# A three-layer decoder on one core: a deeper pipeline for the expert stage, and scatters that wait for products of attention

## The reference

```python
x = x + attn(layernorm(x))          # gated convolution over the 4 batches
x = x + xattn(layernorm(x), ctx)    # linear attention, 16 heads of 64, 128 features
x = x + ffn(layernorm(x))           # 8 experts, top 2
# ffn, for N = 2048 rows of 128:
routing = softmax(xf @ router_w.T); top_w, top_i = top_k(routing, 2)
top_w = top_w / sum(top_w)
h = silu(xf @ w_gate[e].T) * (xf @ w_up[e].T)     # 256 wide
out[n] = sum over the 2 chosen e of top_w * (h @ w_down[e].T)
```

## Time and profile before

| | |
|---|---|
| time, median of 3 runs | 307.88 us (306.1 to 310.2) |
| profiled execution, its own time | 305.2 us |
| its span, first to last instruction | 303.5 us |
| PE / PEld busy | 259.3 us (85%) / 221.1 us (73%) |
| DVE / ACT / POOL busy | 186.3 us (61%) / 162.4 us (54%) / 124.5 us (41%) |
| mean granted TensorE clock | 0.939 of full speed |

### The profile page before, as it was taken

How to read it: one execution, slowest core, us unless ns; L and a number is a source line. 1 busy time by engine, 2 the same in 40 slices (tenths; PEclk the granted TensorE clock), 3 DMA queues, 4 the chain that set the end, 5 groups by cost and what they waited for, 6 DMA issues and landing times.

```text
span 303.5 us, 5721 instructions
## 1 busy us (share of the span) xinstructions
PE 259.3 (85%) x1697; PEld 221.1 (73%) x1697; DVE 186.3 (61%) x713; ACT 162.4 (54%) x343; POOL 124.5 (41%) x183
## 2 busy tenths in 40 slices
PE   6999999999999999997999699778971899889700
PEld 3858686776889998995999488667861899889700
DVE  4678678696588888884888398757650222222206
ACT  2565564655777777773777366342530555445400
POOL 4648999441010001054104510711567466556520
PEclk9999999999999999999799979959996799999965
DMA  7999999940040000001000100257661688674048
GB/s 200 267 216 184 178 181 181 183 56 2 1 138 2 2 1 1 2 26 44 3 0 29 45 1 2 81 159 218 180 201 53 162 241 256 196 220 119 32 142 281
DMA packets 38446, 34.05 MB, mean 112 GB/s; under 512 B 3581, under 2 KB 31234, under 8 KB 38288
## 3 DMA queue, kind: packets, MB, share of 16 engines
q1 hardware_dynamic: 35312, 28.96, 43.3%
q0 software_dynamic: 2272, 4.24, 4.0%
q10 hardware_dynamic: 832, 0.49, 0.6%
HBM read 19.80 MB, written 14.32 MB: 112 GB/s over the span
## 4 chain that ended last, share of the span: by engine, by line
PE 68%; DVE 11%; issue 7%; another core or an unknown queue 5%; DMA 3%; POOL 2%; ACT 2%; ACTq 0%; POOLq 0%; DVEq 0%; SPq 0%
PE num L1294 15%; PE bank L1381 8%; PE num L1391 5%; PE bank L1255 5%; PE num L1233 4%; PE bank L246 4%; PE bank L248 4%; DVE X L929 4%; PE bank L247 4%; PE num L246 3%; PE num L248 2%; PE num L247 2%; PE bank L1166 2%; PE bank L1197 2%
## 5 line engine op out<-in xcount | busy, mean ns | idle before, releaser
L1294 PEld LDWEIGHTS num<-kvw_sb,q 128*128 128x128 f32 x512 | 70.3, 200 | 15.3 <-issue 8.6
L929 DVE SCALAR_TENSOR_TENSOR X<-num,rden,X 128x128 f32<-128x128 f32 x256 | 75.8, 342 | 4.6
L1294 PE MATMUL num<-kvw_sb,q 128*128 128x130 f32 x512 | 72.0, 286 | 7.0 <-DVE X L929 6.9
L666 ACT ACTIVATE relu_z<-bank 128x512 f32<-128x512 f32 x64 | 38.1, 595 | 32.6 <-PE bank L248 19.5
L546 POOL DMA_INDIRECT dispatched<-rows,slot_i x32 | 31.3, 977 | 51.1 <-DVE slot_i L1010 41.5
L566 POOL DMA_INDIRECT expert_out<-yo,xb x39 | 38.1, 977 | 29.2 <-issue 17.3
L1117 DVE TENSOR_TENSOR hid<-bank,silu_g 128x256 f32<-128x256 f32 x39 | 16.4, 422 | 51.2 <-ACT silu_g L694 31.2
L1381 PE MATMUL bank<-xT,wgu_sb 128*128 128x128 f32 x312 | 42.9, 282 | 2.3 <-issue 1.9
L583 ACT ACTIVATE q<-relu_z 128x512 f32<-128x512 f32 x64 | 40.4, 632 | 6.7 <-DVE acc L844 0.8
L1381 PEld LDWEIGHTS bank<-xT,wgu_sb 128*128 128x128 f32 x312 | 39.0, 196 | 3.0 <-issue 2.9
L1391 PE MATMUL num<-wd_sb,hid 128*128 x156 | 25.7, 288 | 12.0 <-issue 7.2
(11 more groups left out here) (173 smaller groups left out, 414.3 us busy)
## 6 DMA issues: line engine op xcount, KB each, us to landing
wgu_sb<-in_wgu SPq DMA_DIRECT2D x39, 256.0 KB
dispatched<-pad_row SPq DMA_DIRECT2D x3, 2795.0 KB, 35.4
xb<-dispatched SPq DMA_DIRECT2D x39, 65.0 KB
y_back<-expert_out SPq DMA_DIRECT2D x4, 512.0 KB, 4.9
wd_sb<-in_wd SPq DMA_DIRECT2D x1, 1024.0 KB, 4.8
out<-X SPq DMA_DIRECT2D x4, 256.0 KB, 2.5
X<-in_x SPq DMA_DIRECT2D x3, 256.0 KB, 6.6
expert_out<-yo,xb POOLq DMA_INDIRECT x39
```

The source lines that it names most:

```text
L666: a.activation(relu_z[:, k % 2, :], z_bank[k % 2], ACT.Relu).then_inc(relu_done, 1)
L929: ins = v.scalar_tensor_tensor(tile_of(n, t), banks[:, t // 2, t % 2, 0:P], rden[:, f % 2, t:t + 1], tile_of(n, t), ALU.mult, ALU.add)
L1294: last = nc.tensor.matmul(num[:, 2 * (h % 2) + t // 2, HA * (t % 2):HA * (t % 2 + 1)], q[:, h % 4, part], kvw_h, start=True, stop=True)
```

## The change

It has two parts.

**Scatters beside attention.** Each of the eight scatters of a round now waits for a product of attention: `after_head` waits either for the features of a head (`z_full`) or for the numerators that follow them (`num_done`). The half steps are counted from head 14 of batch n for the rounds of batches 0 and 1 (so the last ones fall into heads 0 to 3 of the next batch), and from head 10 for batch 2; PACE gives the half step of each scatter. The round of batch 3, in the expert stage, has no such wait, as before.

**Experts.** The gate and up products get two banks up to block 7 and four from block 8 on; the down products of block s come at tick s + 5 instead of s + 2 from block 4 on, and catch up at the end, where four ticks hold two each. The rows of up to four blocks are turned together and copied by one ScalarE instruction (TURNS: tick, first block, blocks; 16 groups instead of 39 instructions). `xT` and `hid` have eight buffers, `silu_g` four, `xb` and `yo` 24. SP loads rows further ahead. Within a tick the order on every engine is now gate and up, down, turning.

```diff
-XRING = 16
+XRING = 24
+DEEP = 4
...
-        SCATTER = (10, 11, 12, 13)
+        SCATTER_HEAD = (10, 14)
+        PACE = (0, 1, 3, 5, 6, 8, 9, 11)
...
+        TURNS = [(0, 0, 1), (0, 1, 1), (1, 2, 1), (2, 3, 1), (3, 4, 2), (5, 6, 2), (7, 8, 4), (11, 12, 4),
+                 (15, 16, 1), (16, 17, 1), (17, 18, 2), (19, 20, 4), (23, 24, 4), (27, 28, 4), (31, 32, 4), (35, 36, 3)]
+        def down_tick(s):
+            if s < 4:
+                return s + 2
+            return min(s + 5, 35 + (s - 30) // 2) if s >= 30 else s + 5
+        down_at = [max(down_tick(s), s + 2) for s in range(RUN)]
+        TICKS = RUN + 2
+        def gu_bank(s):
+            return bank[s % 2] if s < RING else (bank[0], bank[1], o_bank, t_bank)[s % DEEP]
...
+        def pipeline(turn, gate_up, down, beside, before_tick=lambda t: None):
+            for t in range(TICKS):
+                before_tick(t)
+                if 1 <= t <= RUN:
+                    gate_up(t - 1)
+                for s in range(RUN):
+                    if down_at[s] == t:
+                        down(s)
+                for g, (at, _, _) in enumerate(TURNS):
+                    if at == t:
+                        turn(g)
+                for step in beside.get(t, ()):
+                    step()
...
+            def after_head(n, half):
+                f = n * H + half // 2
+                if half % 2:
+                    pool.wait_ge(num_done, f - LAG + 1)
+                else:
+                    pool.wait_ge(z_full, f + 1)
+            def scatters(n, m):
+                first = 2 * SCATTER_HEAD[m < NB - 2]
+                for i in range(TOPK * TPB):
+                    after_head(n, first + PACE[i])
+                    scatter(m, i // TOPK, i % TOPK)
...
-            pipeline(pool, [(2, send)], beside={5: [lambda t=t: scatter(NB - 1, t) for t in range(TPB)]})
+            for s in range(RUN):
+                if s == 4:
+                    for i in range(TOPK * TPB):
+                        scatter(NB - 1, i // TOPK, i % TOPK)
+                send(s)
...
             def gate_up(s):
                 pe.wait_ge(ld_wgu[s % WRING], s // WRING * 16 + 16)
-                pe.wait_ge(xT_done, s + 1)
-                wait_past(pe, hid_done, s - 1)
+                pe.wait_ge(xT_done, turn_of[s] + 1)
+                if s < RING + 2:
+                    wait_past(pe, hid_done, s - 1)
+                elif s == RING + 2:
+                    pe.wait_ge(route, NB * ROUTE_STEPS + 1)
+                elif s == RING + 3:
+                    pe.wait_ge(y3T_done, NB)
+                else:
+                    pe.wait_ge(hid_done, s - DEEP + 1)
```

More of the change, by code:

```diff
@@ L268, in decoder_kernel @@
         FIRST = 3
[L269 to L271 removed]
+        PE_MIXER, PE_Y2, ACT_Y2, DVE_Y2 = 2, 6, 6, 3
+        SCATTER_HEAD = (10, 14)
+        PACE = (0, 1, 3, 5, 6, 8, 9, 11)
         HALVES = 2
@@ L305, in wait_alone, with nothing @@
                 eng.sem_inc(waits_passed, 1)
[L307 to L331, removed]
+        def pipeline(turn, gate_up, down, beside, before_tick=lambda t: None):
[11 more added lines that the diff above has]
+                    step()
+        def nothing(s):
+            pass
         @block.sync
@@ L396, in _ @@
                 load_rows(s - 1)
-            load_rows(WRING - 1)
+            read_rows(WRING, WRING + AHEAD)
+            for s in range(WRING - 1, WRING + AHEAD):
+                load_rows(s)
             for s in range(WRING, EARLY):
-                if s % AHEAD == 0:
-                    read_rows(s, s + AHEAD)
-                load_rows(s)
+                if s == WRING:
+                    read_rows(WRING + AHEAD, EARLY)
                 load_weights(s)
+                if s + AHEAD < EARLY:
+                    load_rows(s + AHEAD)
             sp.wait_ge(table_step, ROWS_LATE)
-            read_rows(EARLY, EARLY + XRING)
+            read_rows(EARLY, EARLY + 16)
             for s in range(EARLY, EARLY + 2):
@@ L544, in scatter, with send @@
                     wait_alone(pool, route, m * ROUTE_STEPS + ROUTE_STEPS + 1)
[L545 to L560, removed]
-            over_batches(pool, attention, last_routing)
-            def send(s, j, turn):
+                g.indirect_dma_start(
+                    out=xs, out_offset=bass.IndirectOffsetOnAxis(ap=slot_i[:, m % 2, t, k:k + 1], axis=0),
+                    in_=rows[:, m % 2, k, t, :], in_offset=None).then_inc(sent[m % 2], 16)
+            def after_head(n, half):
[9 more added lines that the diff above has]
+                    scatter(m, i // TOPK, i % TOPK)
+            for n in range(1, NB):
+                if n == 1:
+                    ln2(NB - 1)
+                third_norm(n - 1)
+                scatters(n, n - 1)
+            third_norm(NB - 1)
+            def send(s):
                 wait_alone(pool, yo_done, s + 1)
@@ L1133, in last_places @@
                     step(NB - 1)
-            pipeline(dve, [(1, hidden)], beside={
+            pipeline(nothing, hidden, nothing, {
                 2: [last_norm],
```

95 lines of the change are left out of this document (54 added, 41 removed).

## The result

The changed kernel takes **300.97 us** (median of 6 runs, 297.83 to 303.2) against 308.07 us (6 runs, 306.1 to 310.2) for the kernel before in the same comparison; the ratio of the comparable runs is 0.971, 95% interval 0.966 to 0.976. The forecast was 293.5 in a range of 286 to 302: the direction was right and the time lies inside, but the gain is 7 to 9 us (by the medians or by the ratio) and not 14.4. The runs of the changed kernel stand in two groups, three from 297.8 to 299.2 and three from 302.7 to 303.2; the profiled execution (302.7 us, span 300.0) is of the upper one, and the ratio is made of the lower one.

The account below looks back on a forecast made before the run. TensorE bounds both stages outside stalls, which come from its signals arriving late behind GpSimd's indirect DMAs. 305.2 - 8 - 6 = 291.2 us; with the median 0.9% higher 293.8, stated as 293.5, range 286 to 302.

Parts of the forecast that it names:

- B: Rival, experts: the new stage gives nothing, since sends behind scatters keep signals late or DMA sets the pace; 299.9 us, chance 0.18.
- A: Rival, attention: the scatters' waits cure nothing, lateness comes after five issues whatever GpSimd does; 301.9 us, chance 0.12.
- That TensorE's signals come late while GpSimd issues: Beside scatter rounds: other engines see TensorE's signals late until GpSimd stops; a relu came over 4 us late.
- five issues without a gap: On GpSimd: about five indirect DMAs issued without a gap were said to start the lateness of TensorE's signals.
- The waits cost nothing in free running: Scatters beside attention: without stalls, their products come before the scatters would start of themselves, so cost is 0.
- The cover of 4.2 us: Round one: 4.2 us between the last scatter's end and `third_norm`'s first instruction, said to hide GpSimd's waits.
- Part 1, 8 us: Scatter waits beside attention: gain 8 us, rounds one (3.5) and two (4.6) nearly whole, 1 of the third; bounds 0 and 11.1.
- Heads 4 to 15 within 1 us of each other: Sign in attention: heads 4 to 15 of batches 1 and 2 should take times within 1 us of each other.
- Part 2, 6 us: Expert stage: 7.4 us gained, 1.8 lost at the end, net 5.6 taken as 6; bounds 0 and 12.
- The step at the fourth round: Experts, scatters back to back: TensorE runs gate and up products ahead, two blocks by the stall, perhaps two more in it.
- steady part: Experts after the fourth round: five ticks of distance swallow signals 1 or 2 us late; included in the 7.4 us gain.
- tail: End of experts: nine downs in six ticks, GpSimd sending each 1.27 us ends some 3.9 us behind TensorE; costs 1.8 us.

Follow-up runs that it names:

- part 2 alone: Changed kernel without the scatters' waits beside attention, block 16 turned at tick 16 instead of 15: 310.71 us against 311.89 for the kernel before, ratio 0.995.

## Why the prediction was right, and where it was wrong

The direction was right, and by the mechanism forecast for part 1. That the time lies inside the range is owed to its width: it was drawn to take in B and A's centre, and what happened in the expert stage is B's mechanism and not the forecast's. By the forecast's own sign of being wrong, late signals that remain and a spacing of 1.6 or more, B came true.

**That TensorE's signals come late while GpSimd issues** holds on the chips where the kernel takes 308 and 312 us: relus wait up to 4.5 us there in the kernel before, up to 6.6 in part 2 alone, and none over 1.2 us on a prompt chip for the same code. Without waits the stalls are all there, and with them GpSimd pauses and they shrink. That five issues without a gap bring it on does not hold as a rule: in the experts it comes back after bunches of three sends, with pauses of 2 us between them (row 243.10 and those around it), and on three chips eight in a row bring on nothing. Whether GpSimd's DMAs are the cause, or its being busy, wasn't shown.

**"The waits cost nothing in free running"** is wrong by 1.0% (2.6 us by the medians) on a prompt chip. The step compared the waits with slots at 131.15 and found half step 0 met by 0.7 us; in round three it is the wait that ends last (11.66 us, put down to the feature product), which the forecast had only in passing ("later than it started before") and didn't price. The cover of 4.2 us ahead of `third_norm` was itself part of the stall: in the kernel before on a prompt chip it is 0.86 us in round one and none in round two.

**Part 1, 8 us**: 7.3 us by the first turning, so the sum held on a late chip. Its terms did not. The prompt chip shows what each round had to give: 3.5, 4.2 and 4.8 us. Round one was to be cured nearly whole and gained 1.3, since six scatters are under way before a wait can hold one back. Round two gained 2.9. The third, taken at 1 us with a bound of 3, gained 2.7 (25.24 to 22.50); the bound was too low. That terms too high and a term too low add up to nearly 8 is luck. "Heads 4 to 15 within 1 us of each other" was missed (22.04 against 19.84); "first expert product near 199" came at 200.01; "no relu idle over 2 us" came at 2.1. No clock below 0.9 between 140 and 190 us: right.

**Part 2, 6 us, is the step that failed**: by the profile the experts take 3.6 us longer. It divides in three.

The step at the fourth round was right in kind: before, block 12 came 34.0 us after the first turning (207.32 to 241.34); now it comes at 229.58, 29.6 us after it, a gain of 4.4.

The *steady part* was wrong: "five ticks of distance swallow a signal that is 1 or 2 us late". From block 14 at 233.96 to block 38 at 277.25 there are 24 steps in 43.29 us, 1.80 each, where 1.45 was forecast and 1.69 stood before. From block 12 to block 38 it is 47.7 us against 43.6, which gives back 4.1, some of it still the half clock behind the round. The five ticks lie between gate and up and down. Two other distances were left as they were: rows are turned one gate and up product ahead of the one that needs them, and in that time ScalarE must weigh and copy, and a down product waits for the weighing of the second before it. From 233.96 to 277.25 TensorE stops six times, 5.3 us in all: four times (3.7 us) before the first product of a group of turned rows, at 241.42, 245.30, 252.45 and 259.03, and twice (1.6 us) before a down product.

The *tail*, 1.8, is 4.0 here: from block 38's gate and up product to the last send it is 8.60 us against 4.61. But it isn't the backlog of sends that was forecast: the last two down products each waited for a late signal (2.04 and 2.39 us), and GpSimd ended 286.82 - 284.67 = 2.15 us behind TensorE, not 3 to 5. Where nothing is late, the last send falls back by about the tail that was forecast, 1.7 us.

In all 4.4 - 4.1 - 4.0, the 3.6 us of loss. All this is of the profiled execution. The three lower runs, near 298.5, were not profiled; if part 1 gave 7.3 in them too, part 2 gave some 2 us (308.1 - 298.5 - 7.3), an estimate, and still not 6. On the second occasion its variant gave 0.5%.

So **rival B's mechanism**, sends ready in bunches with late signals behind them, so that the expert stage gives nothing, fits what happened. The rows show the two following each other; that the bunches keep the signals late was argued, not tested on a late chip. B's time, 299.9, and A's, 301.9, are both within 1.1 us of the median of 300.97, so the time doesn't choose between them; the relus do, against A. B had a chance of 0.18. That the trace showed late signals at 267.21 long after the round was the evidence for it, and I weighed it too low.

**What wasn't in any rival**: that the lateness itself could be absent, and that a stage ahead of its input gains nothing. On prompt chips TensorE arrives at block 16 before its rows, in the kernel before by 2.53 us and with part 2 by 3.98. In the profile of before the fourth round's stall hid how near that bound was. The forecast also weighed instruction fetch. By the Trainium skill, "Runtime: NRT & Kernel Launch", section "Instruction fetch mechanics", the blocks are fetched strictly in order and their cost is mostly hidden. No run here tests it; that the same code has no such stall in the one profile of before from a prompt chip says that the code alone doesn't bring the stalls.

## What to carry to other kernels

Before tuning against a stall that no wait in the code explains, run the unchanged kernel on another chip: here the stalls were 30 of 308 us and were not there on three chips, and the change made against them cost 3% there. Put a wait where it stops the engine that disturbs together with the one that is disturbed, and place its due time from the trace, since a wait that is met before the lateness begins holds nothing back. When a pipeline is made deeper, look for the distances that stay as they were (here the turned rows, one product ahead) and for the first input that can't come earlier, and count what stands queued behind the instruction that waits for it.

## What the runs showed of the hardware

One kernel, unchanged, takes 277.5 to 278.7 us on three chips and 308 and 312 us on two occasions on others, 11 to 12% apart, with runs of each within about 1 to 2% of their median. No late chip is known to have been used twice, so the occasion isn't ruled out. Instruction lengths are the same (a relu 0.596 us on average on a prompt chip and 0.595 on a late one, a scatter 0.977 on both); what differs is when another engine sees that TensorE is done, 4.2 us after in round one and 5.3 in the fourth, always beside GpSimd's indirect DMAs or within a few us of them. About half of the cost is the wait itself and what it leads to in the attention, the rest among the experts. What in the chip makes it so isn't shown by any run here.
